# A fused decoder layer on one core: head normalisation with fewer vector steps, head values copied by ScalarE, and a new slot table

## The chip, the cores and the metric

The kernel runs on one core of one Trainium2 chip. The metric is device time in microseconds; lower is better. A run gives one time, and the profiled execution has its own time beside the span that its trace covers.

## What is computed

A decoder layer with three parts, each with a norm ahead of it and a residual behind it, on `x` of 16 x 128 x 256 (batch, length, width) in float32. Cut to what matters here:

```python
x = x + mamba(layernorm(x))                  # in_proj, conv, silu, x_proj, scan over 128 steps with 16 states, gate, out_proj
x = x + mlstm(layernorm(x), ctx, ctx)        # 4 heads of 64
x = x + graph_of_6_attentions(layernorm(x))  # each: q, k, v by an edge matrix and a node matrix, 8 heads, softmax

# in mlstm, for each head:
C = (q @ k.T / 8) * D                                      # D: decays, causal
normalizer = maximum(abs(sum(C, -1)), exp(-max_log_D))
h = (C / (normalizer + 1e-6)) @ v
mean = mean(h, -1); var = var(h, -1)
out = (h - mean) * rsqrt(var + 1e-6) * scale
```

## The kernel before

The 16 sequences are handled as 8 groups of two (g0 to g7); a group has 256 rows. Four streams of work are laid into one another, all in float32 but for a few masks:

- **a** (`mamba_in`, 11 steps): first norm (LN1), in_proj in four pieces (steps 2 to 5; ScalarE copies them out, VectorE adds the convolution, L1008), x_proj and its root-mean-square norm (steps 7 and 8), dt_proj and softplus (steps 9 and 10).
- **u** (108 steps): the scan in 16 units. Unit k is `feed` (VectorE multiply, L1036, writes a ring of three buffers), `dec` twice (ScalarE exponentials, L824), `scan` (VectorE, L1043), `weigh` (VectorE multiply, L1052) and `add` (TensorE sums over states into a bank, L525). After four units, `gather` (L1060, L1062) closes a chunk of channels.
- **x** (16 steps): the mLSTM. `ml` 0 to 4 are out_proj with the second norm (LN2), the gates and their rows. For each head h, `hs` makes scores (TensorE L579, L580, L582), decays (ScalarE L858) and their product (VectorE L1098); `hv` multiplies by the values (TensorE L589) and copies the result and the row sum out of PSUM into `hrow` (L1104). All four heads share one bank, so TensorE begins head h + 1 only when head h has been copied (`h_read`). `norm` divides by the normalizer and normalises each head (L1113 to L1128). `out` adds the residual, makes the third norm (LN3), transposes it and writes `node` (ScalarE L871).
- **f** (67 slots): the six attention nodes. `k`, `q`, `v` project; `max` makes scores (L651) and VectorE takes row maxima (L1142, `mx`); `score` makes them again less the maxima (L656, L659, L664), and ScalarE takes the exponentials (L897); `edge` is L691, `attend` L676/L678 with the denominators on ScalarE (L906, L907) and the division on VectorE (L1151, `aT`); `node` is L698 and ScalarE L912. `out` is the last norm (LN4).

In a full round TensorE works on nodes of group i, while x of group i + 1, u of group i + 2 and a of group i + 3 go along. One list, `ORDER`, sets the order on all engines: every step has a slot (`A_AT`, `U_AT`, `X_AT`) counted in slots of f, 67 to a group, and each engine walks the sorted list and issues its part of each step, in order. A slot of -10 in `U_AT` means slot 57 of the group before. The weights are prepared once, before the first node (`prep`, 18 steps with slots `P_AT`: three to a node, of which the first has the large products L451 and L459, and each third step lets SyncE load the next weights); `warm` steps (`W_AT`) are matmuls on zeros. `A_SH` and `U_SH` shift the first groups.

The norms share `layer_norm`: means and variances (L977, L981), then one VectorE instruction that adds the constant under the root (L983), then ScalarE's logarithm and exponential (`rstd_of`, L731 and L732), then the scaling (L986). `Chain` counts a semaphore up where an engine waits for its own results.

## Time and profile before

| | |
|---|---|
| median of 3 runs | 1247.11 us (1245.56 to 1249.92) |
| profiled execution | 1245.05 us, span of its trace 1243.0 us |
| mean granted TensorE clock | 0.940 of 2.4 GHz |
| TensorE busy | 1108.4 us, 89% |
| VectorE busy | 987.5 us, 79% |
| ScalarE busy | 733.2 us, 59% |

Busy time says how long an engine had instructions under way. The chain that ended last follows each wait back to what released it; its shares say on which engine the time was spent in which nothing else could have helped (TensorE 57%, VectorE 15%, ScalarE 8%, "issue" 5%). The nodes of the first group begin 213 us into the span; before that lie the preparation and the first groups' a, u and x.

### The profile page before, as it was taken

What the parts mean: (1) busy time and instruction counts of PE and PEld (TensorE: products, weight loads), DVE (VectorE), ACT (ScalarE), POOL (GpSimd) and SP (SyncE); (2) the same over time, 40 slices, a digit from 0 to 9 for tenths busy, and PEclk for the clock granted to TensorE, in tenths of its full rate; (3) what the DMA queues carried; (4) which work ended last, traced back from release to release, by engine and by line L of the source; (5) the groups of instructions that cost most, each with busy time, mean ns of one, the idle gap of its engine ahead of it and who ended that gap; (6) DMA issues with size and microseconds to landing.
All of it is one profiled execution on the core that took longest, in us unless ns stands there. A gap on an engine that the chain in (4) does not pass through costs nothing.

```text
span 1243.0 us, 27121 instructions
## 1 busy us (share of the span) xinstructions
PE 1108.4 (89%) x11540; PEld 839.4 (68%) x11540; DVE 987.5 (79%) x1249; ACT 733.2 (59%) x1725; POOL 15.0 (1%) x31
## 2 busy tenths in 40 slices
PE   7866788999899998999899989999999988998886
PEld 6643556776676777777676767667776766776675
DVE  3499876899889988999899989998998989635222
ACT  3435442876577656776487647765676655544443
POOL 4000000000000000000000000000000000000000
PEclk9867766999999999999999989999999989998998
DMA  6721703022110402041113101131104010000000
GB/s 200 229 106 44 232 10 119 36 63 86 34 60 3 137 35 69 3 137 35 35 37 108 64 10 60 23 116 44 52 2 137 35 61 1 2 2 10 2 1 9
DMA packets 52792, 76.09 MB, mean 61 GB/s; under 512 B 13696, under 2 KB 37504, under 8 KB 52672
## 3 DMA queue, kind: packets, MB, share of 16 engines
q1 hardware_dynamic: 51968, 73.81, 18.6%
q8 instruction: 90, 1.47, 0.5%
q0 software_dynamic: 704, 0.56, 0.2%
q14 instruction: 30, 0.25, 0.1%
HBM read 62.55 MB, written 10.75 MB: 59 GB/s over the span
## 4 chain that ended last, share of the span: by engine, by line
PE 57%; DVE 15%; ACT 8%; issue 5%; DVEq 0%; ACTq 0%
PE ps L620 7%; PE heads L630 6%; PE ps L698 6%; PE ps L691 4%; PE heads L651 4%; PE ps L601 4%; PE heads L659 3%; PE ps L525 3%; DVE ring L1043 3%; PE ps L492 3%; DVE mx L1142 2%; PE ps L549 2%; PE ps L582 1%; PE ps L579 1%; PE ps L676 1%
## 5 line engine op out<-in xcount | busy, mean ns | idle before, releaser
L1043 DVE TENSOR_TENSOR_SCAN ring<-dec,ring 128x1024 f32<-128x1024 f32 x128 | 292.1, 2282 | 0.0
L824 ACT ACTIVATE dec<-dts,a_neg 128x254 f32<-128x254 f32 x512 | 215.3, 498 | 19.5 <-DVE ring L1043 13.6
L1036 DVE TENSOR_TENSOR ring<-dtus,bs 128x1024 f32<-128x1024 f32 x128 | 155.1, 1217 | 3.9 <-DMA dtus<-th 2.0
L1052 DVE TENSOR_TENSOR ring<-ring,cs 128x1024 f32<-128x1024 f32 x128 | 155.9, 1218 | 1.3
L1142 DVE TENSOR_REDUCE mx<-heads 128x16 f32<-128x2048 f32 x48 | 109.7, 2285 | 56.5 <-PE heads L651 55.7
L897 ACT ACTIVATE pr<-heads 128x512 f32<-128x512 f32 x192 | 99.1, 602 | 39.9 <-PE heads L664 39.9
L698 PE MATMUL ps<-aT,wo_f 128*128 128x256 f32 x384 | 100.3, 404 | 15.7 <-DVE aT L1151 15.4
L525 PE MATMUL ps<-ring,fold 128*32 128x256 f32 x1024 | 89.1, 416 | 20.8 <-DVE ring L1052 20.1
L691 PE MATMUL ps<-node,we_f 128*128 128x256 f32 x384 | 99.9, 405 | 0.0
L620 PE MATMUL ps<-node,wq_f 128*128 128x256 f32 x384 | 94.9, 390 | 3.4 <-ACT node L912 3.4
L698 PEld LDWEIGHTS ps<-aT,wo_f 128*128 128x128 f32 x384 | 74.2, 198 | 33.6 <-DVE aT L1151 23.5
L630 PE MATMUL heads<-wv_f,node 128*128 128x256 f32 x384 | 93.7, 387 | 0.0
L620 PEld LDWEIGHTS ps<-node,wq_f 128*128 128x128 f32 x384 | 69.7, 189 | 27.2 <-ACT node L912 18.5
L691 PEld LDWEIGHTS ps<-node,we_f 128*128 128x128 f32 x384 | 73.9, 200 | 13.5 <-issue 0.8
L630 PEld LDWEIGHTS heads<-wv_f,node 128*128 128x128 f32 x384 | 70.4, 190 | 16.2 <-issue 7.9
L601 PE MATMUL ps<-node,wk_f 128*128 128x256 f32 x320 | 79.8, 392 | 0.0
L877 ACT ACTIVATE qT<-ps,fb 128x256 f32<-128x256 f32 x96 | 40.3, 471 | 51.7 <-PE ps L620 50.7
L651 PE MATMUL heads<-kT,qT 32*128 32x128 f32 x1536 | 56.3, 282 | 16.1 <-ACT qT L877 12.0
L492 PE MATMUL ps<-th,win 128*128 128x256 f32 x256 | 63.9, 394 | 7.2 <-ACT u L765 5.7
L601 PEld LDWEIGHTS ps<-node,wk_f 128*128 128x128 f32 x320 | 57.5, 189 | 17.5 <-issue 9.8
L651 PEld LDWEIGHTS heads<-kT,qT 32*128 32x128 f32 x1536 | 48.2, 186 | 30.0 <-issue 30.0
L912 ACT ACTIVATE node<-ps,fb 128x256 f32<-128x256 f32 x96 | 40.1, 469 | 36.9 <-PE ps L698 36.9
(180 smaller groups left out, 1756.3 us busy)
## 6 DMA issues: line engine op xcount, KB each, us to landing
dts<-dt_rows SPq DMA_DIRECT2D x31, 512.0 KB, 3.9
dtus<-dt_rows SPq DMA_DIRECT2D x31, 512.0 KB, 5.2
node<-in_w_edgeT SPq DMA_DIRECT2D x18, 256.0 KB, 3.3
bs<-bc_rows SPq DMA_DIRECT2D x32, 128.0 KB, 5.1
cs<-bc_rows SPq DMA_DIRECT2D x32, 128.0 KB, 5.3
dt_rows<-dt SPq DMA_DIRECT2D x32, 128.0 KB, 2.4
dt_rows<-th SPq DMA_DIRECT2D x32, 128.0 KB, 2.4
xin<-in_x SPq DMA_DIRECT2D x8, 256.0 KB, 3.0
```

What stands on the lines that cost most here:

```text
L525: last = mm(MY[SD * blk:SD * (blk + 1), 0:T], fold[:], ring[(i * UNITS + k) % RING][:, blk, :], start=(q == 0), stop=(q == NGRP - 1), tile ...
L601: last = mm(bank[:, a * T:(a + 1) * T], w[:, k, a * P:(a + 1) * P], src[:, k, :], start=(k == 0), stop=(k == HC - 1))
L620: last = mm(FA[:, a * T:(a + 1) * T], wq_f[c][:, k, a * P:(a + 1) * P], src[:, k, :], start=(a == 0 and k == 0), stop=(k == HC - 1), skip_ ...
L630: last = mm(X3[:, b * H:(b + 1) * H], node[SLOT[GRAPH[c]["v"]]][:, k, b * L:(b + 1) * L], wv_f[c][:, k, :], start=(k == 0), stop=(k == HC ...
L651: last = mm(heads[:, h, to], qT[at], kT[c % 2][at], start=True, stop=True, tile_position=(FD * h, 0))
L691: mm(ED[:, a * T:(a + 1) * T], we_f[c][:, k, a * P:(a + 1) * P], src[:, k, :], start=(a == 0 and k == 0), stop=False, skip_group_check=True)
L698: last = mm(ED[:, a * T:(a + 1) * T], wo_f[c][:, k, a * P:(a + 1) * P], aT[:, k, :], start=False, stop=(k == HC - 1), skip_group_check=True)
L824: last = fn(dec[k % 2][:, blk, :, 1:L], dts[c % 2][:, blk, :].rearrange("p (b t) -> p b t", b=GB)[:, :, 1:L], ACT.Exp, scale=a_neg[:, c, b ...
L1036: v.tensor_tensor(ring[(i * UNITS + k) % RING][:], dtus[c % 2][:], bs[:, q:q + 1, :].broadcast_to([P, BLKS, T]), ALU.mult).then_inc(sig["i ...
L1043: v.tensor_tensor_scan(states, dec[k % 2][:].rearrange("p k b t -> p (k b t)"), states, 0.0, ALU.mult, ALU.add).then_inc(sig["state"], 1)
L1052: v.tensor_tensor(states[:], states[:], cs[:, q:q + 1, :].broadcast_to([P, BLKS, T]), ALU.mult).then_inc(sig["outflow"], 1)
L1142: v.tensor_reduce(mx[:].rearrange("p (h s) -> p h s", h=HPC)[:, :, 0:STEPS], heads[:].rearrange("p h (s k) -> p h s k", s=STEPS), AX.X, AL ...
```

## The change

Four things change.

1. The head norm. Before, `hrow` (8 x 64 values per partition) was multiplied by the inverse denominator (L1117), and the mean was scaled (L1119) before it was subtracted. Now the values stay undivided: the mean's factor goes into the subtraction, and the variance is multiplied by the squared inverse denominator (`den2`, 8 values), and the root by the inverse denominator again (8 values).
2. The constants under the four norms' roots go as the bias of ScalarE's logarithm, which reads the variance from where it lies. L983 and L1164 fall away.
3. The copies of the heads' values (L1104) move from VectorE to ScalarE, in the same slots.
4. The tables `A_AT`, `U_AT`, `X_AT`, `P_AT`, `W_AT` and `A_SH` are new.

```diff
-A_SH = [-244, -12, 1, 1, 1, 1, 1, 1]
+A_SH = [-275, -12, 1, 1, 1, 1, 1, 1]
...
-            def rstd_of(chain, var_sig, done_sig, i, dst):
+            def rstd_of(chain, var_sig, done_sig, i, dst, var=None, eps=0.0):
                 after(act, var_sig, i, 1)
-                chain.link(fn(dst, dst, ACT.Ln))
+                chain.link(fn(dst, dst if var is None else var, ACT.Ln, bias=eps))
                 fn(dst, dst, ACT.Exp, scale=-0.5).then_inc(sig[done_sig], 1)
...
+            def head_values(i, h):
+                after(act, "h_ps", i, h + 1)
+                fn(hrow[:, :, h, :], ML[i > 0][:, 0:GB * XP].rearrange("p (b d) -> p b d", b=GB), ACT.Copy
+                   ).then_inc(sig["h_read"], 1)
...
                 for b in range(GB):
-                    m = chain.mark(v.bn_aggr(mean_var[:, b, :], stats[:, b, :]))
-                chain.wait(m)
-                v.tensor_scalar(inv[:], mean_var[:, :, 1], eps, None, ALU.add).then_inc(sig[f"ln_var{n}"], 1)
+                    last = v.bn_aggr(mean_var[:, b, :], stats[:, b, :])
+                last.then_inc(sig[f"ln_var{n}"], 1)
...
-            def head_values(i, h):
-                after(dve, "h_ps", i, h + 1)
-                v.tensor_copy(hrow[:, :, h, :], ML[i > 0][:, 0:GB * XP].rearrange("p (b d) -> p b d", b=GB)
-                              ).then_inc(sig["h_read"], 1)
...
                 m_chain.link(v.reciprocal(den[:], den[:]))
-                m_chain.link(v.tensor_tensor(hn, hn, den[:].unsqueeze(2).broadcast_to(wide), ALU.mult))
+                m_chain.mark(v.tensor_tensor(den2[:], den[:], den[:], ALU.mult))
                 m_chain.link(v.tensor_reduce(hmu[:], hn, AX.X, ALU.add))
-                m_chain.link(v.tensor_scalar(hmu[:], hmu[:], 1.0 / XD, None, ALU.mult))
-                m_chain.link(v.tensor_tensor(hn, hn, hmu[:].unsqueeze(2).broadcast_to(wide), ALU.subtract))
+                m_chain.link(v.scalar_tensor_tensor(hn, hmu[:].unsqueeze(2).broadcast_to(wide), -1.0 / XD, hn, ALU.mult,
+                                                    ALU.add))
                 m_chain.link(v.tensor_tensor(hsq, hn, hn, ALU.mult))
                 m_chain.link(v.tensor_reduce(hva[:], hsq, AX.X, ALU.add))
-                v.tensor_scalar(hva[:], hva[:], 1.0 / XD, HEAD_EPS, ALU.mult, ALU.add).then_inc(sig["hvar"], 1)
+                v.scalar_tensor_tensor(hva[:], hva[:], 1.0 / XD, den2[:], ALU.mult, ALU.mult).then_inc(sig["hvar"], 1)
                 after(dve, "hrstd", i, 1)
+                m_chain.link(v.tensor_tensor(hva[:], hva[:], den[:], ALU.mult))
                 m_chain.link(v.tensor_tensor(hn, hn, hva[:].unsqueeze(2).broadcast_to(wide), ALU.mult))
```

In `U_AT` the steps `ch 2`, `add 4` and `dec 12` of the next group go from slot -10 to -4, -4 and -3, that is from before the last head's scores (`hs 3`, slot 57) to behind the last node's attention.

Three places show what the tables move.

**ScalarE, from the last node of one group to the first of the next.** L731/L732 are LN3's root, L912 the last node's result, `dec` the decays, L871 the transposed LN3 that the next group's first node reads, L754 LN1's transpose. Before:

```order
L731 ACTIVATE mrstd<-mrstd 128x2
L732 ACTIVATE mrstd<-mrstd 128x2
L912 ACTIVATE node<-ps,fb 128x256 x2
L824 ACTIVATE dec<-dts,a_neg 128x2x127 x2
L871 ACTIVATE node<-ps 128x512
L731 ACTIVATE frstd<-frstd 128x2
```

Now (line numbers are those of the changed file, up to six higher):

```order
L732 ACTIVATE mrstd<-mmv 128x2
L733 ACTIVATE mrstd<-mrstd 128x2
L918 ACTIVATE node<-ps,fb 128x256 x2
L825 ACTIVATE dec<-dts,a_neg 128x2x127 x4
L877 ACTIVATE node<-ps 128x512
L732 ACTIVATE frstd<-fmv 128x2
```

Four decay instructions stand between the last node and the next `node`, where two stood.

**VectorE, at the first node of a group.** L1172 ends the last group's output, then come feed 7 and scan 6 of u, the convolution (`u<-hs_pad`), weigh 6 and the row maxima of node 0. Before:

```order
L1172 SCALAR_TENSOR_TENSOR aT<-aT,frstd,xr 128x256 x2
L1036 TENSOR_TENSOR ring<-dtus,bs 128x1024
L1043 SCALAR_TENSOR_TENSOR ring<-dec,ring 128x1024
L1008 SCALAR_TENSOR_TENSOR u<-hs_pad,vec,u 128x256 x6
L1052 TENSOR_TENSOR ring<-ring,cs 128x1024
L1142 TENSOR_REDUCE mx<-heads 128x4x4
L1036 TENSOR_TENSOR ring<-dtus,bs 128x1024
```

Now:

```order
L1173 SCALAR_TENSOR_TENSOR aT<-aT,frstd,xr 128x256 x2
L1041 TENSOR_TENSOR ring<-dtus,bs 128x1024
L1013 SCALAR_TENSOR_TENSOR u<-hs_pad,vec,u 128x256 x6
L1048 SCALAR_TENSOR_TENSOR ring<-dec,ring 128x1024
L1057 TENSOR_TENSOR ring<-ring,cs 128x1024
L1041 TENSOR_TENSOR ring<-dtus,bs 128x1024
L1143 TENSOR_REDUCE mx<-heads 128x4x4
```

The convolution has moved ahead of scan 6, and the maxima behind scan 6 and feed 8. On TensorE the in_proj piece that this convolution needs (step 2 of a, L492) now stands ahead of node 0's queries (L620) and no longer behind them.

**TensorE, at group 0's gates, before the first node.** L561 makes the gates, L525 is add 1 of group 1, L451 and L459 are the weights' preparation for node 4, L568 transposes the gate rows. Before:

```order
L561 MATMUL ps<-ctxT,wgate 36x256 x2
L525 MATMUL ps<-ring,fold 32x256 x4
L451 MATMUL heads<-node 128x256 x4
L451 MATMUL heads<-qT,node 128x256 x4
L451 MATMUL heads<-kT,node 128x256 x4
L459 MATMUL heads<-vec,node 128x1 x4
L459 MATMUL heads<-vec,qT 128x1 x4
L459 MATMUL heads<-vec,kT 128x1 x4
L568 MATMUL ps<-cst,ml_buf 128x4 x4
```

Now:

```order
L452 MATMUL heads<-kT,node 128x256 x4
L460 MATMUL heads<-vec,node 128x1 x4
L460 MATMUL heads<-vec,qT 128x1 x4
L460 MATMUL heads<-vec,kT 128x1 x4
L526 MATMUL ps<-ring,fold 32x256 x4
L569 MATMUL ps<-cst,ml_buf 128x4 x4
L580 MATMUL ps<-ml_buf,negid 128x256
```

The preparation no longer stands behind add 1; add 1 stands behind it.

## Rows read from the trace of the kernel before

**Rows 1.** Busy time by stretch: stretch, its length, PE, PEld, DVE, ACT, POOL; then clock

```profile
477.00:610.00 133.00, 123.86 (x1394) 93.76 (x1394) 121.84 (x151) 89.93 (x216) 0.00 (x0) 0.99 0.18 57
1008.00:1127.00 119.00, 108.32 (x1247) 82.51 (x1251) 82.38 (x102) 63.34 (x156) 0.00 (x0) 0.96 0.05 15
```

**Rows 2.** The chain that ended last, 530 to 553 us: start, length, what

```profile
531.49 2.17 issue
...
550.54 2.21 DVE mx L1142
```

**Rows 3.** Groups of instructions by form: count | busy us, mean ns | idle before them

```profile
L1043 DVE TENSOR_TENSOR_SCAN ring<-dec,ring 128x1024 f32<-128x1024 f32 x128 | 292.1, 2282 | 0.0
...
L1052 DVE TENSOR_TENSOR ring<-ring,cs 128x1024 f32<-128x1024 f32 x128 | 155.9, 1218 | 1.3
...
L894 ACT ACTIVATE mxT<-ps 128x128 bf16<-128x128 f32 x48 | 13.2, 274 | 15.4 <-PE ps L656 15.4
...
L1104 DVE COPY hrow<-ps 128x130 f32<-128x130 f32 x32 | 8.9, 279 | 12.5 <-PE ps L589 12.3
...
L1117 DVE TENSOR_TENSOR hrow<-hrow,den 128x512 f32<-128x512 f32 x8 | 5.5, 692 | 0.3
...
L983 DVE TENSOR_SCALAR mrstd<-mmv 128x2 f32<-128x2 f32 x16 | 2.7, 169 | 0.5
...
L1114 DVE TENSOR_TENSOR den<-den,em 128x8 f32<-128x8 f32 x8 | 1.3, 167 | 0.3
```

**Rows 4.** Timeline at a group's border, 594 to 611 us: start, length, instruction, idle before

```profile
594.32 0.64 PE L525 MATMUL ps<-ring,fold 128*32 128x256 f32 x8
...
598.37 0.29 DVE L1104 COPY hrow<-ps 128x130 f32<-128x130 f32 x1 [0.75 <-PE ps L589]
...
605.98 3.05 PE L698 MATMUL ps<-aT,wo_f 128*128 128x256 f32 x8 [2.34 <-DVE aT L1151]
...
608.75 0.74 DVE L986 TENSOR_SCALAR hrow<-xr,mmv,mrstd 128x256 f32<-128x256 f32 x2 [0.51 <-ACT mrstd L732]
...
609.07 0.84 ACT L912 ACTIVATE node<-ps,fb 128x256 f32<-128x256 f32 x2 [0.36 <-PE ps L698]
...
609.80 0.90 ACT L824 ACTIVATE dec<-dts,a_neg 128x254 f32<-128x254 f32 x2
...
610.60 0.59 ACT L871 ACTIVATE node<-ps 128x512 f32<-128x512 f32 x1
```

**Rows 5.** Busy time by stretch, columns as in rows 1

```profile
606.00:609.00 3.00, 3.00 (x8) 1.96 (x8) 2.28 (x8) 0.41 (x2) 0.00 (x0) 0.63 0.00 0
```

**Rows 6.** Timeline at a group's first node, 481 to 495 us

```profile
481.06 1.89 PE L620 MATMUL ps<-node,wq_f 128*128 128x256 f32 x8
...
482.79 1.89 PE L492 MATMUL ps<-th,win 128*128 128x256 f32 x8
...
486.38 2.47 DVE L1008 SCALAR_TENSOR_TENSOR u<-hs_pad,vec,u 128x256 f32<-128x256 f32 x6 [1.76 <-ACT u L765]
...
490.14 2.29 DVE L1142 TENSOR_REDUCE mx<-heads 128x16 f32<-128x2048 f32 x1
...
494.17 0.27 PE L656 MATMUL ps<-cst,mx 128*128 128x128 f32 x1
```

**Rows 7.** Timeline before the first node: the first feeds, then group 0's heads

```profile
52.95 2.36 DVE L1036 TENSOR_TENSOR ring<-dtus,bs 128x1024 f32<-128x1024 f32 x2 [2.01 <-DMA dtus<-th]
...
161.72 0.64 PE L525 MATMUL ps<-ring,fold 128*32 128x256 f32 x8 [0.91 <-DVE ring L1052]
...
174.86 0.42 DVE L1098 SCALAR_TENSOR_TENSOR ml_buf<-ps,ml_buf 128x256 f32<-128x256 f32 x1 [2.48 <-ACT ml_buf L858]
...
183.43 1.12 PE L589 MATMUL ps<-vaug,ml_buf 128*128 128x65 f32 x4 [0.24 <-DVE ml_buf L1098]
...
185.82 0.29 DVE L1104 COPY hrow<-ps 128x130 f32<-128x130 f32 x1
...
195.94 0.42 DVE L1098 SCALAR_TENSOR_TENSOR ml_buf<-ps,ml_buf 128x256 f32<-128x256 f32 x1 [3.51 <-PE ps L582]
...
209.32 1.86 PE L439 MATMUL heads<-fb,aT 128*128 128x1 f32 x8 [2.41 <-DVE fb L962]
```

More of the change, by code:

```diff
@@ L93 @@
 P_STEPS = [("p", "prep", n) for n in range(3 * NODES)]
-A_AT = [-100, -69, -67, -66, -64, -63, -59, -58, -55, -44, -41]
-U_AT = [-41, -40, -40, -40, -38, -32, -32, -32, -32, -32, -32, -32, -32, -28, -28, -26, -25, -25, -25, -25, -24,
[4 rows of a table removed]
-X_AT = [24, 37, 41, 42, 45, 47, 49, 51, 53, 55, 56, 57, 57, 59, 63, 64]
-P_AT = [-375, -372, -372, -355, -301, -192, -92, -67, -63, -54, -39, -32, -22, -18, -14, -5, -3, 0]
-A_SH = [-244, -12, 1, 1, 1, 1, 1, 1]
+A_AT = [-100, -69, -68, -66, -65, -63, -63, -58, -47, -44, -42]
+U_AT = [-37, -37, -37, -37, -37, -37, -32, -32, -32, -32, -32, -30, -30, -29, -28, -28, -25, -25, -25, -25, -24,
[4 rows of a table added]
+X_AT = [24, 37, 41, 42, 45, 46, 49, 51, 53, 55, 56, 57, 57, 59, 63, 64]
+P_AT = [-404, -400, -396, -366, -325, -187, -87, -67, -65, -51, -34, -32, -23, -18, -17, -3, -3, 0]
+A_SH = [-275, -12, 1, 1, 1, 1, 1, 1]
 U_SH = [-14, 1, 1, 1, 1, 1, 1, 1]
@@ L117 @@
 W_STEPS = [("w", "warm", n) for n in range(24)]
-W_AT = [-356, -356, -336, -335, -279, -267, -257, -190, -180, -154, -142, -142, -130, -130, -130, -128, -127,
-        -127, -122, -112, -98, -77, -55, -49]
+W_AT = [-450, -333, -333, -333, -324, -324, -316, -302, -262, -223, -187, -162, -159, -157, -155, -155, -142,
+        -134, -125, -100, -73, -61, -16, -11]
 ORDER += [(at, 5, 0, n, step) for n, (step, at) in enumerate(zip(W_STEPS, W_AT))]
@@ L159 @@
     rows_ps=1, rows_read=1, ln_var4=1, ln_rstd4=1, out_ready=1,
-    vec_a=12, vec_m=26, vec_f=5, act_a=4, act_m=5, act_f=2 * NODES + 1,
+    vec_a=10, vec_m=22, vec_f=3, act_a=4, act_m=5, act_f=2 * NODES + 1,
 )
@@ L240, in build @@
         den = sb("den", [P, GB * XH])
+        den2 = sb("den2", [P, GB * XH])
         hmu = sb("hmu", [P, GB * XH])
@@ L747, in mamba_in @@
                     a_chain.start(i)
-                    rstd_of(a_chain, "ln_var1", "ln_rstd1", i, rstd[:])
+                    rstd_of(a_chain, "ln_var1", "ln_rstd1", i, rstd[:], mv[:, :, 1], LN_EPS)
                 if step == 1:
@@ L835, in mlstm @@
                 if step == 1:
-                    rstd_of(m_chain, "ln_var2", "ln_rstd2", i, mrstd[:])
+                    rstd_of(m_chain, "ln_var2", "ln_rstd2", i, mrstd[:], mmv[:, :, 1], LN_EPS)
                 if step == 2:
@@ L915, in ffn_out @@
             def ffn_out(i, _):
-                rstd_of(f_chain, "ln_var4", "ln_rstd4", i, frstd[:])
+                rstd_of(f_chain, "ln_var4", "ln_rstd4", i, frstd[:], fmv[:, :, 1], OUT_EPS)
                 f_chain.end()
@@ L972, in prep, with layer_norm @@
                     dve.sem_inc(sig["w_used"], 1)
-            def layer_norm(i, chain, n, src, mean_var, stats, inv, eps, dst):
+            def layer_norm(i, chain, n, src, mean_var, stats, inv, dst):
                 for b in range(GB):
@@ L997, in mamba_in @@
                         dve.wait_ge(sig["dtu_first"], 16 * BLKS)
-                    layer_norm(i, a_chain, 1, lambda b: xin[:, b, :], mv, bn, rstd, LN_EPS, rows).then_inc(sig["ln1_rows"], 1)
+                    layer_norm(i, a_chain, 1, lambda b: xin[:, b, :], mv, bn, rstd, rows).then_inc(sig["ln1_rows"], 1)
                 if step in (3, 4):
@@ L1136, in mlstm_out @@
                 after(dve, "x2_ready", i, 1)
-                layer_norm(i, m_chain, 3, lambda b: xi[:, b, :], mmv, mbn, mrstd, LN_EPS, mrow).then_inc(sig["ln3_rows"], 1)
+                layer_norm(i, m_chain, 3, lambda b: xi[:, b, :], mmv, mbn, mrstd, mrow).then_inc(sig["ln3_rows"], 1)
                 m_chain.end()
@@ L1161, in ffn_out @@
                 for b in range(GB):
-                    m = f_chain.mark(v.bn_aggr(fmv[:, b, :], fbn[:, b, :]))
-                f_chain.wait(m)
-                v.tensor_scalar(frstd[:], fmv[:, :, 1], OUT_EPS, None, ALU.add).then_inc(sig["ln_var4"], 1)
+                    last = v.bn_aggr(fmv[:, b, :], fbn[:, b, :])
+                last.then_inc(sig["ln_var4"], 1)
+                after(dve, "ln_var4", i, 1)
                 for b in range(GB):
```

10 lines of the change are left out of this document (5 added, 5 removed), and 8 rows, old and new, of the table U_AT.

## The prediction

> **What bounds the kernel now.** I read four views in this order. Busy time by stretch first: in a full group's 133 us TensorE has 123.86 us of work at a clock of 0.99 and VectorE 121.84 [rows 1]. Both are nearly full, so neither is the bound everywhere; a microsecond taken from VectorE is worth something only in the stretches where VectorE is what the others wait for. The chain of waits shows those stretches. From 531.49 to 552.8 it lies on VectorE (row maxima, scans, softplus' tail, LN1, row maxima again) [rows 2], and the reader should see that its pieces abut: VectorE has no slack there. The second such stretch is the group's border, read from the timeline: from the last head's copy at 598.37 everything up to the transposed LN3 at 610.60 (L871) hangs on VectorE and two short ScalarE steps, and TensorE sits idle 2.34 us ahead of L698 [rows 4]. Between these two stretches and from the first node to 531 the chain is TensorE's own work with short ScalarE pieces. So I price each edit twice: what it takes from VectorE's busy time, and what it takes from these two stretches.
>
> **VectorE's work.** A group loses four copies of 279 ns, one multiply of 692, the mean's scaling and four constants, five instructions of about 169, and gains two small ones of 167 [rows 3]: 1.12 + 0.69 + 0.85 - 0.33 = 2.3 us less. The subtraction and the variance's last step only change their form, with the same elements; I price them at nothing, and if the new form cost a tenth more, that would be 0.07 us.
>
> **The border.** Three things shorten it. The head norm on the path loses 0.69 and 0.17 and gains 0.17 twice, with some 0.03 between dependent instructions on both sides: 0.55 less. LN3 loses L983, 0.17 with its gap 0.2. And the last head starts sooner: add 4 (0.64 of TensorE [rows 4]) stood ahead of its scores and now stands behind the attention, inside TensorE's idle time. The scores then reach VectorE 0.5 to 0.6 sooner; VectorE is held until then by node 5's maxima, which leaves 0.45. The copy itself goes from VectorE to ScalarE. No row shows ScalarE copying 130 elements out of PSUM; the nearest is L894 with 128 elements in 274 ns against VectorE's 279 [rows 3]. I take them as equal (0 per copy); ends: 0.1 quicker, and up to 0.3 slower where ScalarE is in another instruction when the product lands. Together LN3's result comes 1.2 sooner than the 608.75 of [rows 4].
>
> The Trainium skill speaks against such a move: "ScalarE: Activation LUTs" (Rules for kernel authors) sends adds, multiplies and the like to VectorE and budgets about 0.3 us plus 0.83 ns an element for an ACTIVATE, 0.41 us for 130. By that the one copy on the path would cost 0.13 more, 0.9 us over the kernel; L894's 274 ns disagrees, and I go by the row.
>
> But the next node waits for L871 on ScalarE, and ScalarE's list has changed just there. Before, L912 began at 609.07 and took 0.84, two decays 0.90, and L871 could start at 610.60 [rows 4]. Now four decays stand between, about 1.7. L698 begins at 605.0 in place of 605.98. How long it takes depends on the clock: at 606 to 609 the granted clock was 0.63 [rows 5], most of it at the lower level, 1.2 GHz, and the eight matmuls took 3.05 where the eight of L620 took 1.89 [rows 4, 6]. With the idle time cut from 2.34 to 0.7 (0.98 sooner, 0.64 filled by add 4) I take the full clock, 1.99: L698 ends at 607.0, L912 waits for LN3's root on ScalarE and runs 607.6 to 608.45, the decays to 610.15, so L871 is **0.45** sooner. At the lower clock it is not sooner at all. Of the 1.2 us won on VectorE, 0.75 is lost to the decays.
>
> **The first node.** The in_proj piece that the convolution needs now runs 1.73 sooner on TensorE (482.79 - 481.06), so the convolution can begin at 484.6 in place of 486.38 [rows 6]. Scan 6 (2.28) used to fill VectorE's wait for it and now comes behind it, so its time is added to what follows. The row maxima now come behind convolution 2.47, scan 2.28, weigh and feed 1.14 each (start to start, of 1.22 busy): 491.7 in place of 490.14, done at 493.9. L656 takes them at 494.17 [rows 6], so 0.2 of slack is left. Until the attention's division the balance is -1.76 for the earlier convolution, +2.28 for the scan, and about -0.8 for a wait of the division on ScalarE that is now filled by work: -0.3 for the second half of `aT`, but the first half comes 0.4 later, and L698 needs both halves in turn. I take **0**; bounds -0.3 and +0.5.
>
> **LN1 and LN2** lie in the VectorE stretch and right behind it, and each loses 0.2: **0.4**. The other moved slots lie where TensorE works without a gap; there they only change who waits. If TensorE's cover fell away there, VectorE's queue would show.
>
> So a full group gains 0.45 + 0.4 + 0 = 0.85. Six groups (g0 to g5) have such a border: 5.1. The seventh has no decays at its border and gains all 1.2 and LN2's 0.2: 1.4. The last gains LN4's constant, 0.2. Sum 6.7.
>
> **Before the first node.** Here ScalarE is mostly idle and VectorE bounds. LN1 twice and LN2 once: 0.6. Node 4's preparation used to wait for add 1 (0.91 idle and 0.64 [rows 7]); now add 1 stands behind it: 1.3 sooner for the gate rows, and so for head 0's product at 174.86. Then each head needs the copy before TensorE goes on. Head 1's values ended at 184.55 (183.43 + 1.12) but the copy began at 185.82, behind a scan: 1.27 late; ScalarE would have taken it at once. The next copy was 0.9 late likewise, and add 4 (1.1 at this clock) stood ahead of head 3. Against that, weigh 2 and feed 4 now come behind head 0's product and not ahead of it, 2.3 us more VectorE work inside the heads. Between 174.86 and 195.94 VectorE has waits, the longest of 3.51 [rows 7], so most of that finds room. I take 2.0 of the 3.3. Then the head norm and LN3, 0.75, of which L439's wait for `fb` behind LN3 at 209.32 [rows 7] lets all through. Sum 4.65; I take **4.5**. The weights' load for node 1 now starts some 3 us later and so runs into the first group's rows; the first scan waits for those. The first two feeds begin at 52.95 behind a wait of 2.01 for `dtus`, which goes by another queue (GpSimd's) [rows 7]; `dts` and its decays have about that much to spare. I price it at 0, bounds -1 (the softplus chain ahead of it is a little sooner) and +2.
>
> **The sum.** 6.7 + 4.5 = 11.2. The profiled execution took 1245.05 (span 1243.0 and 2.05 around it), so the changed one would take 1233.9. The median of the runs is 2.06 above the profiled execution: 1247.11 - 11.2 = **1236**.
>
> **Rivals.**
> - *VectorE is the bound everywhere.* Its busy share speaks for it. Then each of eight groups gains 2.3 and the start 2 more from its chain: 20, time 1227. Against it: the chain lies on TensorE for more than half the span, and VectorE's 11 us of idle per group are waits for others.
> - *Only the start gains.* ScalarE's queue takes the border's gain (L698 stays at the lower clock, or the copies wait behind decays) and the first node's VectorE list runs 0.5 late, so that LN1 and LN2 are spent: a full group gains nothing, 4.5 + 1.6 less some loss in the first load: 3 to 6, time 1243.
> - *The row maxima of node 0 come too late.* Slack is 0.2 [rows 6]. It decides when VectorE's stretch from the convolution is longer than I have it, say because the convolution waits for ScalarE (queries' and keys' copies stand there too). Each microsecond beyond the slack costs one per group, seven times, less the 1.6 per group gained elsewhere. With 2.5 us late: 7 x (2.3 - 0.85) - 6 = +4, time 1251, slower.
> - *The norm is not shorter.* The new forms with a repeated operand might run slower than the plain ones (692 ns a piece). At 0.4 us more the border gains nothing: 8 x 0.5 = 4 less, time 1240; that lies inside my range.
>
> **How the numbers follow.** A difference of less than 0.3%, 3.7 us, can't be told from none: the bounds are 1243.4 and 1250.9. Forecast (gain 6 to 16, the norm's rival with it) 0.56; VectorE everywhere 0.13; only the start 0.22, of which a third is beyond 3.7 us; row maxima late 0.07, nearly all slower; no effect at all 0.02. Faster: 0.56 + 0.13 + 0.07 = 0.76; same 0.17; slower 0.07. The range takes in the first rival to 1227 and the second to 1245; what is left out is the third and both tails, about 0.18. The likeliest case's own range is 1231 to 1241.
>
> **What would show it.** Right: no L983 kind left and VectorE about 18 us less busy in all; ScalarE's copies near 0.28 us and 9 us in all; L698 at a group's border behind an idle time under 1.5 us and taking about 2 us; four decays directly ahead of `node` (L877 now) with no idle time before it; a group's period 0.9 us shorter; the first node's keys at 209 rather than 213. Wrong: `mx` of node 0 in the chain of waits with TensorE idle ahead of L657; copies that begin over half a microsecond after their values; `node` waiting for LN3 rather than for the decays, which would mean that the gain is larger; the first feed later than 54.

## The result, and the profile after

The changed kernel took 1248.93 us in the median of 20 runs (1246.94 to 1253.42), the kernel before 1245.41 in 20 runs beside it: ratio 1.0029, 95% interval 1.0018 to 1.0040. It is 0.3% slower, 3.5 us, where 0.9% faster was forecast. The profiled execution took 1248.32 us, 3.3 more than the 1245.05 of before.

The page of the changed kernel, the busy time, the chain that ended last, and the group of the row maxima (busy, mean ns | idle time before them):

```profile
span 1246.5 us, 27088 instructions
...
PE 1116.7 (90%) x11540; PEld 846.4 (68%) x11540; DVE 970.7 (78%) x1185; ACT 740.6 (59%) x1757; POOL 15.0 (1%) x31
...
PE 52%; DVE 21%; ACT 6%; issue 5%; DVEq 0%; ACTq 0%
...
L1143 DVE TENSOR_REDUCE mx<-heads 128x16 f32<-128x2048 f32 x48 | 109.6, 2284 | 71.3 <-PE heads L652 71.3
```

VectorE has 16.8 us less work, as meant. TensorE has the same 11540 matmuls and is busy 8.3 us longer. So the matmuls themselves ran slower, and VectorE now waits longer for them ahead of `mx`: 71.3 us in all, before 56.5.

Where the time went shows in the groups, cut from one `node` copy (L871, now L877) to the next. Columns as in rows 1. The changed kernel:

```profile
212.38:347.32 134.94, 126.98 (x1392) 96.28 (x1390) 115.51 (x133) 90.02 (x216) 0.00 (x0) 0.96 0.16 50
347.32:479.29 131.97, 123.24 (x1392) 94.04 (x1392) 119.62 (x143) 90.26 (x218) 0.00 (x0) 0.99 0.18 57
479.29:611.86 132.57, 123.56 (x1392) 93.97 (x1392) 119.74 (x143) 90.29 (x219) 0.00 (x0) 0.99 0.18 57
611.86:746.91 135.05, 126.37 (x1392) 96.14 (x1392) 119.63 (x143) 90.41 (x219) 0.00 (x0) 0.96 0.18 56
746.91:883.14 136.23, 128.10 (x1392) 97.69 (x1392) 119.79 (x143) 90.42 (x218) 0.00 (x0) 0.95 0.18 56
883.14:1016.28 133.14, 124.95 (x1392) 95.13 (x1392) 118.15 (x137) 90.11 (x216) 0.00 (x0) 0.97 0.18 55
1016.28:1138.84 122.56, 111.56 (x1296) 85.13 (x1297) 82.46 (x101) 64.97 (x164) 0.00 (x0) 0.96 0.04 14
```

The kernel before:

```profile
212.18:345.36 133.18, 125.03 (x1392) 94.32 (x1390) 117.31 (x141) 89.10 (x212) 0.00 (x0) 0.98 0.16 51
345.36:478.14 132.78, 123.97 (x1393) 93.72 (x1392) 121.48 (x151) 89.40 (x215) 0.00 (x0) 0.99 0.18 57
478.14:610.60 132.46, 123.32 (x1392) 93.64 (x1392) 121.30 (x151) 89.39 (x215) 0.00 (x0) 0.99 0.18 57
610.60:744.38 133.78, 125.17 (x1393) 95.15 (x1392) 121.36 (x151) 89.59 (x214) 0.00 (x0) 0.97 0.18 57
744.38:876.85 132.47, 123.71 (x1395) 93.81 (x1394) 121.99 (x152) 89.41 (x214) 0.00 (x0) 0.99 0.18 57
876.85:1010.52 133.67, 125.16 (x1393) 95.20 (x1392) 119.63 (x144) 89.31 (x212) 0.00 (x0) 0.97 0.17 55
1010.52:1133.74 123.22, 111.74 (x1300) 85.09 (x1299) 85.38 (x109) 64.16 (x160) 0.00 (x0) 0.96 0.04 14
```

The column before the last two is the granted clock. At 0.99 the changed kernel's groups take 132.0 and 132.6, before's 132.5 to 132.8: in the mean a gain of 0.3, where 0.85 was forecast. But four of the changed kernel's seven groups have 0.96 or less (before one, the last), and three of these take 135 to 136. The work and the order in the groups from 347 to 883 are the same; they differ by 4.3 us. The seven groups took 926.46 in place of 921.56, and the first of them began at 212.38 in place of 212.18, where 4.5 sooner was forecast. So 11.4 us of the forecast are missing in these groups (6.5 less was forecast, 4.9 more came) and 4.7 before them; from the last `node` copy to the end the kernel took 1.6 less, where 0.2 was forecast.

The border of the changed kernel, from the last head to the next group's `node`:

```profile
598.22 0.90 PE L590 MATMUL ps<-vaug,ml_buf 128*128 128x65 f32 x4 [1.49 <-DVE ml_buf L1103]
...
599.15 0.28 ACT L865 ACTIVATE hrow<-ps 128x130 f32<-128x130 f32 x1 [1.76 <-PE ps L590]
...
599.26 2.09 PE L660 MATMUL heads<-qT,kT 32*128 32x128 f32 x32
...
599.46 0.17 DVE L1113 SCALAR_TENSOR_TENSOR den<-hrow 128x8 f32<-128x8 f32 x1 [1.30 <-ACT hrow L865]
...
601.82 2.07 ACT L903 ACTIVATE pr<-heads 128x512 f32<-128x512 f32 x4 [2.17 <-PE heads L665]
...
603.74 0.23 ACT L732 ACTIVATE hva<-hva 128x8 f32<-128x8 f32 x1
...
604.25 0.17 DVE L1125 TENSOR_TENSOR hva<-hva,den 128x8 f32<-128x8 f32 x1 [0.80 <-ACT hva L733]
...
606.38 1.99 PE L699 MATMUL ps<-aT,wo_f 128*128 128x256 f32 x8 [0.21 <-DVE aT L1152]
...
609.68 0.73 DVE L991 TENSOR_SCALAR hrow<-xr,mmv,mrstd 128x256 f32<-128x256 f32 x2 [0.51 <-ACT mrstd L733]
...
610.27 1.69 ACT L825 ACTIVATE dec<-dts,a_neg 128x254 f32<-128x254 f32 x4
...
611.86 0.58 ACT L877 ACTIVATE node<-ps 128x512 f32<-128x512 f32 x1
```

And the granted clock there (columns as in rows 1):

```profile
598.00:603.00 5.00, 4.78 (x59) 4.19 (x60) 3.46 (x10) 1.68 (x5) 0.00 (x0) 0.66 0.23 52
```

L699 has the full clock, 1.99, as forecast, and L877 follows the four decays without an idle time. But the stretch at the lower clock has not gone. It moved from behind the wait ahead of L698 [rows 5] to behind the wait of 1.49 ahead of L590, and ended while L692 began (2.08 in place of 1.99).

Set against the group's start (479.29, before 478.14), VectorE has the last head's product 0.59 sooner than before (L1103 at 597.75, L1098 at 597.19). Then the low stretch takes it back. L590 takes 0.90 in place of 0.66. L660 takes 2.09 in place of 1.17; its scores feed the exponentials (L903), and these hold ScalarE 0.28 longer than VectorE needs the root (L732; VectorE waits 0.80 in place of 0.52). The division's second half then waits 0.32 for denominators that come no sooner than before (L913). Another 0.2 is a gap between two small VectorE instructions (L987), which this kernel has at no other border. So LN3's scaling stands at 609.68, that is 608.5 on the clock of before: 0.2 sooner, not 1.2, and L877 behind its four decays 0.1 later, not 0.45 sooner.

Before the first node, the stretch around group 1's in_proj. VectorE of the changed kernel:

```profile
93.94 1.23 DVE L1041 TENSOR_TENSOR ring<-dtus,bs 128x1024 f32<-128x1024 f32 x1 [1.58 <-PE ps L526]
96.40 2.29 DVE L1048 TENSOR_TENSOR_SCAN ring<-dec,ring 128x1024 f32<-128x1024 f32 x1 [1.23 <-ACT dec L825]
```

and of the kernel before:

```profile
91.78 1.22 DVE L1036 TENSOR_TENSOR ring<-dtus,bs 128x1024 f32<-128x1024 f32 x1
92.91 2.28 DVE L1043 TENSOR_TENSOR_SCAN ring<-dec,ring 128x1024 f32<-128x1024 f32 x1
```

VectorE bounds this part, and under the new slots it waits 2.8 us here for `add` and decays that stand behind in_proj. Its first feed, too, began at 54.7 and not at 53.0, and for another reason than before. There it waited for `dtus` [rows 7]; here it follows a step of the weights' preparation in VectorE's own list:

```profile
54.29 0.22 DVE L975 SCALAR_TENSOR_TENSOR fb<-heads,vec,bias_t 128x2 f32<-128x2 f32 x1 [2.42 <-PE heads L440]
54.72 2.36 DVE L1041 TENSOR_TENSOR ring<-dtus,bs 128x1024 f32<-128x1024 f32 x2 [0.21 <-DVE fb L975]
```

That preparation began on TensorE (L452) at 40.96, behind 2.64 us of waiting for the load of `aT`, and its first 8 matmuls took 3.78, at the lower clock. Before, they began at 39.17 without a wait and took 1.99. What `dtus` is loaded from was ready 0.9 sooner than before (L1028 at 43.75, before L1023 at 44.68).

### The profile page after: what moved, and what is told of

It is laid out like the page before. It is cut to its first block, busy times and chain, and to the rows that moved or that the text cites. A ratio compares the mean times of both kernels' runs of the same rounds, so it can differ in the third digit from the quotient of the medians.

```text
span 1246.5 us, 27088 instructions
## 1 busy us (share of the span) xinstructions
PE 1116.7 (90%) x11540; PEld 846.4 (68%) x11540; DVE 970.7 (78%) x1185; ACT 740.6 (59%) x1757; POOL 15.0 (1%) x31
## 4 chain that ended last, share of the span: by engine, by line
PE 52%; DVE 21%; ACT 6%; issue 5%; DVEq 0%; ACTq 0%
PE ps L621 6%; DVE ring L1048 6%; PE ps L699 6%; DVE mx L1143 5%; PE heads L631 5%; PE ps L692 5%; PE heads L660 4%; PE heads L652 3%; PE ps L602 3%; PE ps L526 3%; DVE u L1013 2%; PE ps L550 2%; DVE ring L1041 2%; PE ps L590 1%; PE ps L677 1%
## 5 line engine op out<-in xcount | busy, mean ns | idle before, releaser
L825 ACT ACTIVATE dec<-dts,a_neg 128x254 f32<-128x254 f32 x512 | 218.0, 500 | 12.2 <-DVE ring L1048 8.8
L1143 DVE TENSOR_REDUCE mx<-heads 128x16 f32<-128x2048 f32 x48 | 109.6, 2284 | 71.3 <-PE heads L652 71.3
L903 ACT ACTIVATE pr<-heads 128x512 f32<-128x512 f32 x192 | 99.1, 602 | 43.3 <-PE heads L665 43.3
L699 PE MATMUL ps<-aT,wo_f 128*128 128x256 f32 x384 | 96.0, 391 | 8.1 <-DVE aT L1152 7.4
L692 PE MATMUL ps<-node,we_f 128*128 128x256 f32 x384 | 101.6, 410 | 0.0
L699 PEld LDWEIGHTS ps<-aT,wo_f 128*128 128x128 f32 x384 | 71.6, 192 | 27.0 <-DVE aT L1152 17.5
L692 PEld LDWEIGHTS ps<-node,we_f 128*128 128x128 f32 x384 | 75.3, 204 | 16.4 <-issue 4.3
L602 PE MATMUL ps<-node,wk_f 128*128 128x256 f32 x320 | 82.4, 401 | 0.0
L893 ACT ACTIVATE kT<-ps,fb 128x256 f32<-128x256 f32 x80 | 33.6, 471 | 51.7 <-PE ps L602 51.7
```

The costliest lines, as they stand in the source:

```text
L602: last = mm(bank[:, a * T:(a + 1) * T], w[:, k, a * P:(a + 1) * P], src[:, k, :], start=(k == 0), stop=(k == HC - 1))
L692: mm(ED[:, a * T:(a + 1) * T], we_f[c][:, k, a * P:(a + 1) * P], src[:, k, :], start=(a == 0 and k == 0), stop=False, skip_group_check=True)
L699: last = mm(ED[:, a * T:(a + 1) * T], wo_f[c][:, k, a * P:(a + 1) * P], aT[:, k, :], start=False, stop=(k == HC - 1), skip_group_check=True)
L825: last = fn(dec[k % 2][:, blk, :, 1:L], dts[c % 2][:, blk, :].rearrange("p (b t) -> p b t", b=GB)[:, :, 1:L], ACT.Exp, scale=a_neg[:, c, b ...
L1143: v.tensor_reduce(mx[:].rearrange("p (h s) -> p h s", h=HPC)[:, :, 0:STEPS], heads[:].rearrange("p h (s k) -> p h s k", s=STEPS), AX.X, AL ...
```

## The experiments

The two theories at the start: the edits gain and the new tables lose it again; or there was nothing to gain, since TensorE and its clock bound the groups. A third, that ScalarE's copies cost what the norms save. "Filled" kernels, which put idle matmuls into waits of TensorE, came later. Each row stands against runs of the kernel before on the same chip; the clock is the mean over the kernel's runs (before: 0.940).

| kernel | median us | ratio to before, 95% interval | clock |
|---|---|---|---|
| changed kernel | 1248.9 | 1.0029 (1.0018 to 1.0040) | 0.931 |
| e1 all edits, old tables | 1239.7 | 0.9960 (0.9945 to 0.9975) | 0.941 |
| e2 new tables, old code | 1268.4 | 1.0189 (1.0174 to 1.0204) | 0.926 |
| e3 new groups, old start | 1247.1 | 1.0004 (0.9985 to 1.0022) | 0.936 |
| e7 old groups, new start | 1250.5 | 1.0039 (1.0022 to 1.0055) | 0.935 |
| e9 e1 + A_AT, X_AT new | 1248.7 | 1.0027 (1.0013 to 1.0041) | 0.939 |
| e10 e1 + U_AT new | 1280.4 | 1.0274 (1.0252 to 1.0295) | 0.931 |
| e5 norms' edits only, old tables | 1239.5 | 0.9948 (0.9929 to 0.9966) | 0.940 |
| e6 copies only, old tables | 1243.3 | 0.9988 (0.9972 to 1.0003) | 0.942 |
| h1 as e1, ScalarE copies in group 0 alone | 1238.9 | 0.9950 (0.9931 to 0.9969) | 0.942 |
| f1 changed, dec 12 back | 1243.8 | 1.0003 (0.9991 to 1.0014) | 0.935 |
| f2 e1 + first node's slots | 1239.7 | 0.9960 (0.9944 to 0.9976) | 0.946 |
| g2 changed, filled | 1239.7 | 0.9954 (0.9935 to 0.9973) | 0.947 |
| g3 before, filled | 1237.7 | 0.9944 (0.9923 to 0.9964) | 0.954 |
| g5 f1, filled | 1231.3 | 0.9895 (0.9872 to 0.9919) | 0.950 |
| g4 h1, filled | 1227.0 | 0.9854 (0.9832 to 0.9876) | 0.955 |
| g1 e1, filled | 1227.3 | 0.9847 (0.9819 to 0.9876) | 0.956 |
| g6 g4 + first node's slots | 1229.6 | 0.9870 (0.9845 to 0.9896) | 0.953 |
| g7 g4 + add 4 behind the attention | 1220.4 | 0.9809 (0.9782 to 0.9837) | 0.958 |

**e1: all edits, old tables.** All six tables as before (`A_SH = [-244, ...` in place of `[-275, ...`, and so on), the code as changed.

> All code edits (head norm, norm constants, ScalarE copies), with all six tables of the kernel before. Tables theory (the edits gain, the new slots lose it again): 4 to 8 us faster than the kernel before, about 1239. Nothing-to-gain theory (TensorE's work and its clock bound the groups, less work on VectorE is worth nothing): within 2 us of the kernel before, about 1245. Copies theory (the copies and the norm's steps on ScalarE queue behind exponentials and cost what the norm saves): 2 to 5 us slower, about 1249, as slow as the changed kernel, so that the tables have no part in it.

1239.7, as the first theory has it. The profiled run began its first node at 208.70 (before 212.18) and took 920.8 for the seven groups (before 921.6).

**e2: new tables, old code.** The converse.

> The kernel before with all six tables of the changed one, no code edit. Tables theory: slower than the kernel before by 8 to 12 us, about 1255, and slower than the changed kernel too. Nothing-to-gain theory: about the changed kernel's time, 1248 to 1250. Copies theory: about the kernel before's time, 1245.

1268.4, which no theory had (1255 was the highest expectation). The tables cost the old code 1.9% and the new code 0.7% (1.0029 over 0.9960); in the other direction, the edits are worth 0.4% on the old tables and 1.6% on the new. The effects do not add.

**e3 and e7: start or groups.** `P_AT`, `W_AT` and `A_SH` on one side, `A_AT`, `U_AT` and `X_AT` on the other.

> The changed kernel with P_AT, W_AT and A_SH of before (the preparation's slots, the warm matmuls' and the first groups' shift); the groups' tables stay new. Tables theory, if the loss is in the start (weights' load later, first scan 1.8 us later, the weights' last preparation behind LN3): about 4 us faster than the changed kernel, 1244 to 1245, and the first node's transposed LN3 copy about 208 us into the span in place of 212.4. If the loss is in the groups: within 1 us of the changed kernel, 1248 to 1249.

> The changed kernel with A_AT, U_AT and X_AT of before; P_AT, W_AT and A_SH stay new. If the loss is in the groups: the changed kernel less 5 to 6 us, about 1243, with group periods of 131.6 to 132.5 us at undisturbed clock in place of 132.6. If the loss is in the start: within 1 us of the changed kernel.

Both results miss what was expected (e3 at 1244 to 1245 or 1248 to 1249, e7 at 1243 or as the changed kernel). Each half alone costs time, and the two do not add: e3 lost 7.4 to e1, e7 10.8, both together 9.2. In e3 the first node still began at 212.50. So the start's loss comes with the groups' tables (the same `A_AT` and `U_AT` order the first groups), and the new start alone made it 220.68.

**e9 and e10: which of the groups' tables.**

```diff
-A_AT = [-100, -69, -67, -66, -64, -63, -59, -58, -55, -44, -41]
+A_AT = [-100, -69, -68, -66, -65, -63, -63, -58, -47, -44, -42]
```

> e1_code_old_tables with A_AT and X_AT of the changed kernel (in_proj, x_proj and the convolution's first piece moved; X_AT differs in one slot). If the loss in the groups comes from a's slots: near 1247, as the new groups' tables with the old start gave (1247.1). If it comes from U_AT (add 4 and two decays behind the last node, scan 6 behind the convolution): 1239 to 1241, as e1.

> e1_code_old_tables with U_AT of the changed kernel, all other tables old. If U_AT carries the loss: near 1247, with four decays directly ahead of node's copy at a border and more of TensorE's time at half the clock than in e1. If a's slots carry it: 1239 to 1241. If only the two together (A_AT and U_AT were changed as a pair): over 1250 here or in e9.

`A_AT` alone leaves the groups as they were (920.2 for seven) and delays the first node by 8.8 us. `U_AT` alone takes 138.5 to 141.7 us in each of the first six groups: VectorE waits 4.03 for the convolution's input, which `A_AT` would have brought sooner. The two are one table in effect.

**e5 and e6: norms and copies apart.**

e5 is e1 with `head_values` on VectorE again; e6 is the kernel before with it on ScalarE, as in the third part of the change.

> The tables of before, the head norm's and the norm constants' edits, but the heads' values copied by VectorE as before. Against e1_code_old_tables (1239.7, ratio 0.996) this takes the ScalarE copies away. Mixed theory (the copies help only before the first node, where VectorE bounds, and cost some 0.2 us at each group's border, where VectorE waited 1.23 us for ScalarE's copy instead of 0.75 for TensorE and 0.29 for its own copy): the first node's transposed LN3 copy about 2 us later than in e1 (210.5 against 208.7), seven groups together 1.5 us shorter, time 1239 to 1241. Copies-gain theory: 2 to 4 us slower than e1, 1242 to 1244. Copies-cost theory: 1.5 us or more faster than e1, under 1238.

> The kernel before with one edit, the heads' values copied by ScalarE. Mixed theory: 2 us sooner at the first node (210.2 against 212.2), 0.2 us later at each border, time within 1.5 us of the kernel before. Copies-gain theory: 2 to 4 us faster than before. Copies-cost theory: 1.5 us or more slower.

The norms' edits carry the gain (0.9948); the copies alone are 0.9988, an interval that holds no change. In the profiled runs e5's first node began 2.9 later than e1's, but 1.5 of it was there at the first scan (56.57 and 55.05), which hangs on the load of the first rows. How far such starts scatter can be read from four kernels that are the same up to the first node (e1, h1, g1, g4): it began at 208.70, 207.00, 211.04 and 209.66. So a difference of 2 to 3 us before the first node, in one profiled run each, tells nothing by itself.

**h1: ScalarE's copies in the first group only.**

```diff
             def head_values(i, h):        # on ScalarE
+                if i > 0:
+                    return
                 after(act, "h_ps", i, h + 1)
```

> e1_code_old_tables with the heads' values copied by ScalarE in the first group only and by VectorE in the other seven. In the profiled runs the start took 208.7 us with ScalarE's copies and 211.6 with VectorE's, the seven groups 920.8 and 919.1, the rest 107.7 both. If the two parts add: 1237 to 1238, the fastest of all. If the differences between e1 and e5 are the clock's scatter: 1239 to 1240, as both.

1238.9: between the two expectations, not told from e1 or e5. Its runs spread from 1233.4 (clock 0.948) to 1241.7 (0.937), and that spread hides what was asked.

**f1: dec 12 back.** One number of `U_AT`, -3 to -10.

> The changed kernel with one number of U_AT put back: dec 12 stands before the last head's scores again (slot -10), so that two decays and not four stand between the last node and the transposed LN3 copy (L877). If the decays hold L877 up, as the prediction has it: L877 0.7 us sooner at six borders, periods 0.7 us shorter where the clock is the same (131.3 in place of 132.0), 4 us in all, 1245. If L877 waits for LN3 anyway: no change, 1248 to 1249. If the two decays cost as much in the place they go back to (before the last head, ahead of its exponentials): no change either, but with L877 without a decay before it.

Ratio 1.0003 against 1.0029: 3 us of the 4 expected. It is a sum of several things: in the profiled runs the first node began 2.4 later than in the changed kernel, and the clock was higher (0.937 and 0.932). ScalarE at a border of f1:

```profile
745.82 0.90 ACT L821 ACTIVATE dec<-dts,a_neg 128x254 f32<-128x254 f32 x2
...
746.71 0.60 ACT L873 ACTIVATE node<-ps 128x512 f32<-128x512 f32 x1
```

At clock 0.99 two groups of f1 took 131.46 and 131.80, the changed kernel's 131.97 and 132.57: about 0.5 less. The decays did hold L877 up.

**f2: scan 6 behind the convolution.** e1 with four numbers changed:

```diff
-A_AT: in 2 -67, in 4 -64      U_AT: feed 7 -2, scan 6 -2
+A_AT: in 2 -68, in 4 -65      U_AT: feed 7 -1, scan 6  1
```

> e1_code_old_tables (1239.7) with the first node's part of the tables new: in_proj steps 2 and 4 one slot sooner (A_AT -68, -65), feed 7 at -1 and scan 6 at 1, behind the convolution. The prediction priced this at 0 a group, bounds -0.3 and +0.5: 1237.5 to 1243. If the scan behind the convolution makes node 0's row maxima late: 0.5 to 1.5 us a group more and a wait of TensorE ahead of L657 in node 0, 1243 to 1250. If the earlier convolution pays: under 1237.5.

Equal to e1 at a higher clock (0.946 and 0.941), so the clock may hide a loss; g6 below decides.

**g2: TensorE's waits filled.** By now one thing ran through all results: within a kernel, the longer runs were mostly those with the lower clock. The times and clocks of e3's twelve runs:

```
1240.15 @ 0.941   1240.54 @ 0.940   1241.19 @ 0.939   1241.23 @ 0.942
1242.06 @ 0.937   1247.03 @ 0.935   1247.13 @ 0.932   1247.45 @ 0.931
1248.30 @ 0.935   1248.31 @ 0.930   1249.35 @ 0.934   1249.74 @ 0.931
```

So the clock was tested by itself. `fill(bank, 2)` issues two matmuls on zeros, 1.03 to 1.13 us of TensorE in g2's trace, which counts each of them twice:

```diff
+            def fill(bank, n):
+                for _ in range(n):
+                    mm(bank[:, 0:T], ones[:], zeros[:], start=True, stop=True)
...
+                            if i >= 3:
+                                fill(X1, 2)               # dt_proj, ahead of the second half
                             after(pe, "dt_read", i, 1)
...
+                if i >= 1 and h == XH - 1:
+                    fill(FA, 2)                           # last head's values
                 after(pe, "cT_ready", i, h + 1)
...
+                if i >= 1:
+                    fill(X1, 2)                           # the transposition of LN3
                 after(pe, "ln3_rows", i, 1)
...
+                if c == NODES - 1:
+                    fill(X1, 2)                           # the last node's L699
```

> The changed kernel with two 128x256 matmuls on zeros (some 0.43 us each at full clock) issued into each of four waits of TensorE in a group, into banks that nobody reads then: before dt_proj's second half (wait 1.01), before the last head's values (1.49), before the last node's L699 (1.23), before LN3's transposition (1.36). Clock theory (the changed kernel's groups lose to stretches at the lower clock, and these waits bring the clock down): granted clock 0.945 or more in place of 0.932, fewer low stretches in the groups, 3 to 8 us faster than the changed kernel. Rival (the low stretches don't hang on these waits): clock within 0.003 of 0.932 and time the same or up to 3 us slower, since a fill that meets a low stretch runs past its wait.

0.9954 against 1.0029, 9 us faster, with more work on TensorE; mean clock 0.931 to 0.947. That is the clock theory, a little beyond its 3 to 8 us.

**g3, g5, g4: the same fills on other kernels.**

> The kernel before with the same fills (two matmuls on zeros into each of four waits of TensorE in a group). If the fills work on any kernel: clock above 0.940, 2 to 6 us faster than the kernel before, 1239 to 1243, and the changed kernel with fills (1239.7) then stands against this by the worth of its edits alone. If the kernel before had no low stretches to lose beyond one a group: within 1 us of it or up to 3 us slower, 1245 to 1248, and the fills' gain belongs to the changed kernel's tables alone.

> The changed kernel with dec 12 put back (f1_dec12_back, 1243.8) and the fills. If decays and clock are two separate losses that add: 1243.8 - 9 = 1235. If both act on the same wait (the border's low stretch): 1239 to 1240, as the fills alone.

> h1_copies_by_group (old tables, norms' edits, ScalarE copies in the first group only; 1238.9, clock 0.942) with the fills. Clock theory: clock 0.948 or more, 3 to 5 us faster, 1234 to 1236, the fastest of all. If the fills cost what they win there: 1238 to 1241.

The kernel before gains too, 0.56% or 6 to 7 us, so the waits were a loss of it as well. Filled, the changed kernel is still not faster than the kernel before (0.9954 and 0.9944), so the fills alone do not bring the forecast gain. g4 came out 7 us and g5 4 us under what was expected. Groups in the filled kernels (columns as in rows 1), g3, the kernel before:

```profile
476.64:608.73 132.09, 126.27 (x1410) 95.75 (x1409) 121.62 (x151) 89.32 (x214) 0.00 (x0) 1.00 0.18 57
```

g2, the changed kernel:

```profile
346.51:479.53 133.02, 127.69 (x1408) 96.64 (x1408) 119.65 (x143) 90.28 (x218) 0.00 (x0) 0.99 0.19 57
```

g4, old tables with the norms' edits:

```profile
341.19:472.02 130.83, 126.17 (x1410) 95.75 (x1409) 120.43 (x147) 89.33 (x213) 0.00 (x0) 1.00 0.18 58
```

At an even clock of 1.00 the norms' edits are worth 1.26 us a group (132.09 to 130.83), and from the second group to the sixth a group's time is the same from one to the next within 0.2 us (g3: 132.1 four times, then 131.9). g2 kept one low stretch in each of the first six groups. In four of them it lies in the keys of node 5 (L612 took 3.65 to 3.68 in place of 1.99), with no wait of TensorE over 0.32 us in the 20 us before it; in the other two in the keys of node 0, behind the border's waits. g5, which differs by two decays, has node 5's in one group only. So not every low stretch follows a wait. The two losses, decays and clock, do add: g5 stands 17 us below the changed kernel, more than 3 and 9.

g5 also gives the price of both. Its group with the low stretch takes 132.39, the like group beside it 130.77: 1.6 for the stretch. With the same stretch g2's groups take 133.0, so the two decays cost 0.6. Without it g2's would take some 131.4 (an estimate from these two), 0.7 less than g3's 132.1: close to the 0.85 that was forecast for a group.

**g1, g6, g7: the sum's own terms at an even clock.**

> e1_code_old_tables (all code edits, ScalarE copies in every group) with the fills, beside g4_copies_by_group_filled (1227.0), which differs in the copies of groups 1 to 7 alone. If ScalarE's copies cost 0.2 us or more a group at an even clock: periods of 131.1 in place of 130.85, 1228.5 to 1231. If equal, as predicted (bounds -0.1 and +0.3 a copy): 1226 to 1228.5.

> g4_copies_by_group_filled with the first node's slots of the changed kernel (in_proj steps 2 and 4 one slot sooner, feed 7 at -1, scan 6 behind the convolution), as f2_scan6_behind_conv but at an even clock. Prediction's price: 0 a group, bounds -0.3 and +0.5, so 1225 to 1230.5 against 1227.0. If the row maxima come late: over 1231.

```diff
-U_AT: ch 2 -10, add 4 -10, dec 12 -10
+U_AT: ch 2 -4,  add 4 -4,  dec 12 -10
```

> g4_copies_by_group_filled with add 4 (and ch 2) moved behind the last node's attention as in the changed kernel, dec 12 left where it was. Prediction: the last head starts 0.45 us sooner, seven times, 3 us faster, 1224. If the last head waits for VectorE or ScalarE anyway: 1226 to 1228. If TensorE's wait for the last head's scores grows by what add 4 used to fill and the low stretches return: clock under 0.950 and 1229 or more.

g1's groups take 131.05 where g4's take 130.83, so ScalarE's copies cost 0.22 a group; the whole is not told apart. g6's take 131.04: the new order at the first node costs 0.2. g7's take 130.29 to 130.47, 0.5 less than g4's, and it is the fastest of all, 1220.4, 2% below the kernel before. Not all of its 6.7 us below g4 is the move: its profiled run is 7.5 shorter, of which 3.7 lie in the first six groups, 1.2 in the seventh, and 2.9 before the first node, where starts scatter. Its five runs also lie in two places, 1219.5 to 1220.4 and 1225.1 to 1225.2. VectorE at the last head in g4, whose group began at 472.02:

```profile
590.83 0.42 DVE L1117 SCALAR_TENSOR_TENSOR ml_buf<-ps,ml_buf 128x256 f32<-128x256 f32 x1 [0.45 <-ACT ml_buf L871]
...
601.54 0.74 DVE L1005 TENSOR_SCALAR hrow<-xr,mmv,mrstd 128x256 f32<-128x256 f32 x2 [0.51 <-ACT mrstd L745]
```

and in g7, whose group began at 467.55:

```profile
585.84 0.41 DVE L1113 SCALAR_TENSOR_TENSOR ml_buf<-ps,ml_buf 128x256 f32<-128x256 f32 x1
```

118.81 and 118.29 after the group's start: the head begins 0.52 sooner.

## Why the prediction was wrong, point by point

- **VectorE's work**, 2.3 us less a group, 18 in all: right in the main, 16.8. The new forms cost what the old ones did (L1119, with the repeated operand, has a mean of 692 ns), and the rival "the norm is not shorter" is out.
- **The border's VectorE chain**, 0.55 + 0.2 shorter: right at an even clock. From the last head's copy to LN3's scaling g4 takes 9.53 (the copy at 592.01, L1005 at 601.54), before 10.38 [rows 4] (g3, filled, 10.39). With LN1 and LN2 at 0.2 each that makes the 1.26 of g3 to g4.
- **The last head 0.45 sooner**: right in mechanism and size, 0.52 in g7. The changed kernel had it too, 0.59 at the border shown. But TensorE then lacked add 4 as filling, waited 1.49 ahead of L590 (1.23 before), and ran L590 and L660 at the lower clock, which took the gain back.
- **L698 at the full clock**: it was (1.99). The step that failed is the tacit one behind it, that a low stretch taken from L698 is gone. It fell on L590 and L660, some 6 us earlier, on work that the exponentials, the root and the division wait for. More broadly, **the sum had no term for the clock**: it took the 0.99 of rows 1 for every group of the changed kernel. The profiled clocks of the seven groups were 0.95 to 0.99, and summed over length (length times one less the clock) this comes to 29 us against 20 before, with 8.3 us more busy time on TensorE. That is most of the 11.4 us that are missing in the groups. The fills show that the clock costs time (9 us of the changed kernel in g2), but also that it costs the kernel before 6 to 7; how much of the 3.5 us between the two is the clock's is not shown apart.
- **Four decays cost L877 0.75**: right in place and nearly in size: 0.5 at clock 0.99 in f1, 0.6 between g2 and g5.
- **Copies even on ScalarE, 0, bounds -0.1 and +0.3**: the value was 0.22 a group (g1 against g4), inside the bounds. A copy takes 277 ns on ScalarE (L865, mean of 32) and 279 on VectorE, so it isn't its length. Nor is it the one copy on the path: in g1 VectorE waits 1.06 for it, and g4, where VectorE copies, has 0.75 of waiting and 0.29 of copying. The 0.22 is there before the last head, where VectorE's row maxima wait 0.44 for scores (0.25 in g4); why is open. The Trainium skill ("ScalarE: Activation LUTs", Rules for kernel authors) states its budget, from which the prediction has 0.41 us, for an ACTIVATE whose bias is a pointer operand. These copies give no bias, so the figure is not for them, and their 277 ns do not speak against it.
- **The first node, 0, bounds -0.3 and +0.5**: 0.2 (g6), inside.
- **Before the first node, 4.5**: with the old tables the edits gave 3.5 in e1 (208.70 against 212.18), against 3.35 in the terms that are the edits' (norms 0.6 and 0.75, copies 2.0). That it fits so well is luck: the four kernels with this start lie between 207.00 and 211.04, and apart the norms gave 0.6 (e5) and the copies 0.9 (e6). The slots' own part, 1.3 for node 4's preparation with 0 for the first load, is the step that failed. The new tables took 3.7 against e1 (212.38), 3.3 against the mean of the four. In rows: the first feed 1.8 late, and 2.8 of waiting at 94 to 96. A feed later than 54 was the prediction's own sign of being wrong, and +2 its upper end. But the path was another: not `dtus` or the decays but the preparation of the next weights, which waited for its load, met the lower clock and stood ahead of the feed in VectorE's list. The waiting at 94 to 96 was not looked at, since the slots around group 1's in_proj were passed over.
- **The new tables as a whole** were taken as neutral outside three places. They cost 0.7% (e1 against the changed kernel), 3.7 us before the first node and 5.7 in the groups by the profiled runs; no single table holds the loss (e3, e7, e9, e10). At an even clock the groups' part is no loss but for the decays: g5's groups, new tables with dec 12 back, take 130.8, g1's with the old tables 131.05. I priced the moves that looked useful and let the other fifty stand at zero.
- **The rivals**: "row maxima of node 0 too late" named the right sign for the wrong mechanism. "Only the start gains" had L698 at the lower clock, but neither it nor another had low stretches at new places, or a start that loses.

Still open: why g2 keeps a low stretch in node 5's keys, and how the groups' loss in the kernels without fills divides between moves and clock, since every move shifts where the waits fall.

## What to carry to other kernels

Where the bound engine's clock varies, put it in the sum: read the granted clock of several like stretches, set their lengths side by side, and ask of each edit what wait of that engine it opens. A stretch at the lower clock that is taken from one place may turn up at a worse one. To price small edits at all, first make the clock even, here with idle matmuls in four waits; then terms of 0.2 to 0.5 us a group, which the plain runs could not tell, could be read off. Read the part before the first node apart from the groups: here it scattered by up to 4 us among kernels with the same start. And a new order table is an edit of its own: time it with the old code, and the new code with the old table, before either is believed.
